# A selective scan's rows of B and C spread by DMA, and five of sixteen products with C moved to GpSimd

## The chip, the core and the metric

The kernel runs on one core of a Trainium2 chip. The metric is the device time of one execution in microseconds (us). A core has five engines that each work through their own instruction list in order and wait for each other by semaphores: TensorE (PE), VectorE (DVE), ScalarE (ACT), GpSimd (POOL) and SyncE (SP), which here only issues DMAs. PE writes to PSUM banks; GpSimd works on SBUF alone.

## The reference, cut to what matters

Six layers run one after another over x of shape (8, 512, 128): a two-of-eight expert layer, attention on sine and cosine features, the expert layer again, a routed attention layer with 16 experts, a selective scan (state space layer), and the routed layer again. The change touches the fifth. For a batch of 512 positions, with 256 inner channels d and 16 states n, it computes

```python
deltaA = jnp.exp(jnp.einsum('bld,dn->bldn', delta, A))
deltaB_u = (delta * u)[..., None] * Bm[:, :, None, :]
def step(h, t):
    dA_t, dBu_t, C_t = t
    h = dA_t * h + dBu_t
    return (h, jnp.einsum('bdn,bn->bd', h, C_t))
```

B, C and a low-rank part of delta come from one product: `inputs @ W_x` gives 64 columns for delta, 16 for B, 16 for C. u is a gated depthwise convolution of the input, and the result is y = sum + u * D, times silu of a second half, times W_out.

## The kernel before, in words

In the scan layer (`scan(4)` in each engine's program) channels lie on partitions, in two halves h of 128, and the 512 positions along the free dimension. The work is cut into units: k = 32 b + 2 s + h for batch b, state s, half h, 256 in all. Each engine's program is a loop over a clock U (`SCAN_CLOCK`, L129), and at each step it issues what is due for units near U, so the order of work is written out by hand. For a unit:

- ScalarE makes the decay exp(dt * A) into a PSUM bank (`decay_of`, L788, one unit ahead; banks `decay`, L334, two of them).
- GpSimd makes dB = du * B into a ring of six SBUF tiles (`dB_of`, L531, three units ahead in its list; `DRING`). It waits for the row of B spread over all partitions, and for the scan six units earlier to have used the slot.
- VectorE scans (`scan_of`, L1544: `tensor_tensor_scan`, h = decay * h + dB, from PSUM and SBUF) into a ring of eight tiles `hs` (`HRING`), and one step later multiplies by C (`times_C`, L1537), which lies spread over partitions in a PSUM bank (`C_bank`), into a ring `hc` of eight.
- PE adds hc into the accumulator of its half (bank 4 or 5) by a product with the identity (`sum_of`, L1180), three units later, or at unit 7 of the batch at the earliest (`sum_at`, L147).

Spreading: a batch's rows of B and C are split by VectorE into three bf16 parts (`three_parts`, L1500 to L1504, front step -5), turned by PE and copied (`bcT3`); for each state PE spreads the row of B into bank 2 by a product with `pick` (`spread_B`, L1157), ScalarE copies it to one of four SBUF tiles `Bs` (`copy_B`, L775, `RING`), and PE spreads the row of C into one of two banks (`spread_C`, L1164).

Beside the units run a batch's preparation (`front`, started a batch or more ahead and spread over the clock: norm at step -13, nmr at -11, u at 0 and 12, dt at 15 and 19, g at 22 and 24; all its products pass through bank 7 one after another, `into_bank7`, L1082) and its end (`back`: yg at 4 and 5, the sum into x at 8; on PE the skip product `skip_u` at 5 and 6 and the output product at 6, `OUT7`). On GpSimd the front holds rstd and two products du (steps -12, 17, 21). The code has a constant `ON_POOL` (L124) for states whose product with C goes to GpSimd; it is empty, so `copy_C` (L781) and GpSimd's `times_C` (L541) run for no state.

In the routed layers, SP spreads rows by DMA: it stores 16 rows to DRAM (`rows_to_dram`, L437) and then reads each into all 128 partitions (`widen`, L441, 256 KB each).

Of the kernel before, what the change touches and what calls it, by code (L numbers as in the profile page):

```python
# [25 lines left out]
NB = 8  # L26
# [97 lines left out]
ON_POOL = ()  # L124
# [17 lines left out]
def copies_C(s):  # L142

    return sum(i % NS in ON_POOL for i in range(s))
# [56 lines left out]
def macaron(nc, x, wl, phase, WqT, bq, WkT, bk, Wv, bv, WoT, bo, gateT, expT, W_in, K_conv, b_conv, W_x,  # L201
            W_dt, b_dt, A_log, D, W_out, b_out, sim, gates, wqkv, wo2, out):
    with ExitStack() as ctx:
# [10 lines left out]
        def plain(name):  # L214
# [109 lines left out]
        rows_sb = [t[0:E2, :] for t in (th, thr)]  # L324
        hs = [sb(f"hs{i}", [P, L]) for i in range(HRING - RING)] + xe
# [8 lines left out]
        decay = [bank[0], bank[6]]  # L334
# [11 lines left out]
        rows_out = plain("rows_out")  # L346
        rows_ps, rows_made = sem("rows_ps"), sem("rows_made")
# [30 lines left out]
            bcT_sb, B_ps, B_sb, C_ps, C_sb, dA_made, dB_made, h_made, hc_dve, hc_pool, hc_used, yg_made = (  # L378
                sem(n) for n in ("nmr_made", "bank7_ps", "rows_read", "dlt_sb", "g_made", "th_made", "thr_made", "u_made", "Du_done", "ez_made",
                                 "ln_made", "dt_made", "gates_made", "bc3_made", "bcT_sb", "B_ps", "B_sb", "C_ps", "C_sb",  # L380
# [37 lines left out]
        def _(sp):  # L418
# [31 lines left out]

            for r in range(2):
                sent = 0
# [13 lines left out]
        def _(pool):  # L466
# [52 lines left out]
            def scan(layer):  # L519
# [11 lines left out]
                def dB_of(k):  # L531
# [4 lines left out]
                    pool.wait_ge(B_sb, seen(s + 1))  # L536
# [4 lines left out]
                def times_C(k):  # L541

                    pool.wait_ge(C_sb, seen(copies_C(k // NH + 1)))
                    pool.wait_ge(h_made, seen(k + 1))
                    if k >= HRING:
                        pool.wait_ge(hc_used, seen(SUM_RANK[k - HRING]))
                    pool.tensor_tensor(hc[k % HRING], hs[k % HRING][:], Cs[copies_C(k // NH) % 2], ALU.mult).then_inc(hc_pool, 1)
# [42 lines left out]
        def _(act):  # L590
# [139 lines left out]
            def scan(layer):  # L730
                def front(b):
# [19 lines left out]
                    act.activation(dlt[0:DR, :], bank[7][0:DR, :], ACT.Copy).then_inc(dlt_sb, 1)  # L751
                    yield
# [22 lines left out]
                def copy_B(s):  # L775
                    act.wait_ge(B_ps, seen(s + 1))
                    if s >= RING:
                        act.wait_ge(dB_made, seen(NH * (s + 1 - RING)))
                    act.activation(Bs[s % RING][:], bank[2][:], ACT.Copy).then_inc(B_sb, 1)

                def copy_C(s):  # L781
                    n = copies_C(s)
                    act.wait_ge(C_ps, seen(s + 1))
                    if n >= 2:
                        act.wait_ge(hc_pool, seen(NH * (n - 1)))
                    act.activation(Cs[n % 2], C_bank[s % 2][:], ACT.Copy).then_inc(C_sb, 1)

# [9 lines left out]
                for U in SCAN_CLOCK:  # L797
                    if 0 <= U + 1 < ALL:
                        decay_of(U + 1)
                    if U % 2 and 0 <= (U + 7) // 2 < NB * NS:  # L800
                        copy_B((U + 7) // 2)
                    due(steps, U)
                    if U % 2 and 0 <= U < ALL and on_pool(U):
                        copy_C(U // 2)
# [8 lines left out]
        def _(pe):  # L813
# [267 lines left out]
            def scan(layer):  # L1081
                def into_bank7(name, b):  # L1082
# [11 lines left out]
                    elif last == "dlt":  # L1094
                        pe.wait_ge(dlt_sb, seen(c + 1))
# [5 lines left out]
                def front(b):  # L1101
# [25 lines left out]
                    pe.matmul(bank[7][0:DR, :], wx_sb[:, 0:DR], xpad[:, 1:L + 1], start=True, stop=True).then_inc(bank7_ps, 1)  # L1127
# [29 lines left out]
                def spread_B(s):  # L1157
                    if s % NS == 0:
                        pe.wait_ge(bcT_sb, seen(s // NS + 1))
                    if s:  # L1160
                        pe.wait_ge(B_sb, seen(s))
                    pe.matmul(bank[2][:], pick[:, s % NS, :], bcT3[s // NS % 2][:], start=True, stop=True).then_inc(B_ps, 1)

                def spread_C(s):  # L1164
                    if s >= 2:
                        last = NH * (s - 1) - 1
                        if on_pool(last):
                            pe.wait_ge(C_sb, seen(copies_C(s - 1)))
                        else:
                            pe.wait_ge(hc_dve, seen(products(last + 1, False)))  # L1170
                    pe.matmul(C_bank[s % 2][:], pick[:, NS + s % NS, :], bcT3[s // NS % 2][:], start=True, stop=True).then_inc(C_ps, 1)  # L1171
# [14 lines left out]
                for U in SCAN_CLOCK:  # L1186
                    if U % 2 == 0 and 0 <= (U + 8) // 2 < NB * NS:
                        spread_B((U + 8) // 2)
# [6 lines left out]
                    if 0 <= U + 1 < ALL and U % 2:  # L1195
                        spread_C((U + 1) // 2)
# [9 lines left out]
        def _(dve):  # L1206
# [283 lines left out]
            def scan(layer):  # L1490
# [46 lines left out]
                def times_C(k):  # L1537
                    dve.wait_ge(h_made, seen(k + 1))
                    dve.wait_ge(C_ps, seen(k // NH + 1))
                    if k >= HRING:  # L1540
                        dve.wait_ge(hc_used, seen(SUM_RANK[k - HRING]))
                    dve.tensor_tensor(hc[k % HRING], hs[k % HRING][:], C_bank[k // NH % 2][:], ALU.mult).then_inc(hc_dve, 1)  # L1542
# [54 lines left out]
```

## Time and profile before

| | us |
|---|---|
| median of 3 runs | 1728.18 (1726.42 to 1730.58) |
| profiled execution | 1722.91 |
| its span | 1721.1 |

| engine | busy us | share of span |
|---|---|---|
| PE | 1474.2 | 86% |
| VectorE | 1208.4 | 70% |
| ScalarE | 585.2 | 34% |
| GpSimd | 435.7 | 25% |

Busy shares are means over stages that have different limits, so the scan stage has to be cut out by time. Its first scan starts at 804.3 us and the last at 1350.6 us. Matmuls are pipelined, so a busy PE need not be at its peak. Times in brackets in a timeline row are the engine's idle time just before and what ended it.

### The profile page before, as it was taken

What the parts mean: (1) busy time and instruction counts of PE and PEld (TensorE: products, weight loads), DVE (VectorE), ACT (ScalarE), POOL (GpSimd) and SP (SyncE); (2) the same over time, 40 slices, a digit from 0 to 9 for tenths busy, and PEclk for the clock granted to TensorE, in tenths of its full rate; (3) what the DMA queues carried; (4) which work ended last, traced back from release to release, by engine and by line L of the source; (5) the groups of instructions that cost most, each with busy time, mean ns of one, the idle gap of its engine ahead of it and who ended that gap; (6) DMA issues with size and microseconds to landing.
All of it is one profiled execution on the core that took longest, in us unless ns stands there. A gap on an engine that the chain in (4) does not pass through costs nothing.

```text
span 1721.1 us, 22005 instructions
## 1 busy us (share of the span) xinstructions
PE 1474.2 (86%) x7582; PEld 1070.7 (62%) x7582; DVE 1208.4 (70%) x2729; ACT 585.2 (34%) x1131; POOL 435.7 (25%) x368
## 2 busy tenths in 40 slices
PE   3997885895999999976888878878887589999998
PEld 3894554795899999842343333333332289999996
DVE  3666663665676666424989898898989767676763
ACT  2203443200222222114646556565565212222221
POOL 1130000001000000004656576565666200000000
PEclk9998997897999999976999989998899889999998
DMA  4000000002232333200000000000000043333330
GB/s 131 1 1 1 1 1 1 1 1 99 99 100 99 101 117 110 70 1 1 0 1 1 1 1 1 0 1 0 1 1 1 6 169 112 121 106 105 105 106 13
DMA packets 49581, 76.76 MB, mean 45 GB/s; under 512 B 6775, under 2 KB 15934, under 8 KB 49342
## 3 DMA queue, kind: packets, MB, share of 16 engines
q1 hardware_dynamic: 49470, 75.35, 13.4%
q8 instruction: 60, 0.98, 0.2%
q14 instruction: 51, 0.42, 0.1%
HBM read 72.71 MB, written 2.62 MB: 44 GB/s over the span
## 4 chain that ended last, share of the span: by engine, by line
PE 63%; DVE 15%; issue 13%; ACT 4%; POOL 3%; DMA 1%; DVEq 0%; POOLq 0%; ACTq 0%
PE bank L1057 20%; PE bank L1060 7%; PE bank L914 5%; PE bank L1183 5%; DVE hs L1550 3%; PE bank L950 2%; PE bank L1017 2%; DVE xe L1550 2%; PE bank L1119 2%; DVE both L1542 2%; PE bank L1002 2%; PE bank L1069 2%; POOL both L539 2%; PE bank L999 1%; PE bank L959 1%
## 5 line engine op out<-in xcount | busy, mean ns | idle before, releaser
L1057 PE MATMUL bank<-wqkv_sb,xe 128*128 128x192 f32 x2048 | 370.4, 334 | 10.5 <-DVE xe L1487 10.3
L1057 PEld LDWEIGHTS bank<-wqkv_sb,xe 128*128 128x128 f32 x2048 | 340.1, 194 | 21.9 <-DVE xe L1487 15.4
L1183 PE MATMUL bank<-both,ident 128*128 128x512 f32 x512 | 265.2, 619 | 3.0 <-DVE both L1542 3.0
L507 POOL TENSOR_TENSOR rstd<-ve,half_neg 128x4 f32<-128x4 f32 x32 | 37.5, 1173 | 769.8 <-DVE ve L1238 769.8
L794 ACT ACTIVATE bank<-dt,A 128x512 f32<-128x512 f32 x256 | 174.5, 687 | 145.2 <-DVE xe L1550 95.0
L539 POOL TENSOR_TENSOR both<-du,prob 128x512 f32<-128x512 f32 x128 | 161.6, 1269 | 102.2 <-DVE xe L1550 56.6
L539 POOL TENSOR_TENSOR both<-du,prT 128x512 f32<-128x512 f32 x128 | 161.5, 1271 | 58.8 <-DVE hs L1550 33.8
L1550 DVE TENSOR_TENSOR_SCAN xe<-bank,both 128x512 f32<-128x512 f32 x128 | 155.3, 1213 | 5.5 <-ACT bank L794 5.2
L1550 DVE TENSOR_TENSOR_SCAN hs<-bank,both 128x512 f32<-128x512 f32 x128 | 155.1, 1212 | 2.1 <-ACT bank L794 2.1
L1183 PEld LDWEIGHTS bank<-both,ident 128*128 128x128 f32 x512 | 97.9, 198 | 86.7 <-issue 54.6
L914 PEld LDWEIGHTS bank<-exp_sb,xe 128*128 128x128 f32 x1024 | 138.3, 197 | 5.0
L914 PE MATMUL bank<-exp_sb,xe 128*128 128x128 f32 x1024 | 138.1, 280 | 0.0
L1060 PEld LDWEIGHTS bank<-wo_sb,xe 128*128 128x128 f32 x1024 | 129.7, 192 | 4.2
L1060 PE MATMUL bank<-wo_sb,xe 128*128 128x128 f32 x1024 | 129.8, 275 | 0.0
L1487 DVE TENSOR_TENSOR xe<-at,bank 128x512 f32<-128x512 f32 x128 | 87.6, 686 | 57.9 <-PE bank L1069 57.5
L1370 DVE TENSOR_TENSOR xe<-both,bank 128x512 f32<-128x512 f32 x128 | 86.7, 684 | 50.3 <-PE bank L906 49.1
L1487 DVE TENSOR_TENSOR xe<-xnT,dt 128x512 f32<-128x512 f32 x128 | 85.4, 688 | 22.4 <-DMA dt<-w_rows 15.7
L1457 DVE TENSOR_REDUCE smax<-bank 128x1 f32<-128x128 f32 (+1 forms) x64 | 31.4, 491 | 98.8 <-PE bank L1002 79.7
L1542 DVE TENSOR_TENSOR both<-hs,bank 128x512 f32<-128x512 f32 x128 | 84.6, 661 | 22.9 <-PE bank L1171 11.2
L710 ACT ACTIVATE prT<-bank 128x128 f32<-128x128 f32 (+1 forms) x64 | 28.0, 437 | 192.9 <-PE bank L1009 192.9
L1487 DVE TENSOR_TENSOR xe<-xnT,du 128x512 f32<-128x512 f32 x128 | 84.5, 687 | 9.3 <-PE bank L1057 8.1
L1542 DVE TENSOR_TENSOR both<-xe,bank 128x512 f32<-128x512 f32 x128 | 84.1, 657 | 0.0
(271 smaller groups left out, 2134.5 us busy)
## 6 DMA issues: line engine op xcount, KB each, us to landing
dt<-w_rows SPq DMA_DIRECT2D x128, 256.0 KB, 4.2
du<-w_rows SPq DMA_DIRECT2D x128, 256.0 KB, 4.9
xs<-in_x_dram SPq DMA_DIRECT2D x8, 256.0 KB, 3.7
out_dram<-xs SPq DMA_DIRECT2D x8, 256.0 KB, 2.5
wqkv_sb<-in_wqkv_dram SPq DMA_DIRECT2D x1, 1536.0 KB
exp_sb<-in_expT_dram SPq DMA_DIRECT2D x1, 512.0 KB, 4.9
wo_sb<-in_wo_dram SPq DMA_DIRECT2D x1, 512.0 KB
win_sb<-in_W_in_dram SPq DMA_DIRECT2D x1, 256.0 KB
```

Of the source, the lines that this page charges most:

```text
L507: pool.tensor_tensor(rstd[:], ve[:], half_neg[:, 0:NT], ALU.pow).then_inc(ln_rstd, 1)
L539: pool.tensor_tensor(dB[k % DRING], du[b % 2][:, h, :], Bs[s % RING][:], ALU.mult).then_inc(dB_made, 1)
L794: act.activation(decay[k % len(decay)][:], dt_[b % 2][:, h, :], ACT.Exp, scale=A[:, h, s:s + 1]).then_inc(dA_made, 1)
L914: m = pe.matmul(bank[7 - b % 2][:, j * P:(j + 1) * P], xe[u % RING][:, j * P:(j + 1) * P], exp_sb[:, e, :], start=(e == 0 and j == 0), sto ...
L950: m = pe.matmul(bank[2 + k % 2][:], feat[:, 2 + c, k * P:(k + 1) * P], feat[:, c, :], start=(c == 0), stop=(c == 1))
L1057: m = pe.matmul(bank[4 + j // 2][:, (j % 2) * 3 * HD:(j % 2 + 1) * 3 * HD], x_e, wqkv_sb[:, e, :], start=(e == 0 and j % 2 == 0), stop=(e ...
L1060: m = pe.matmul(bank[7][:, j * P:(j + 1) * P], x_e, wo2_sb[:, e - E2, :], start=(e == E2 and j == 0), stop=(e == UNIT - 1 and j == NT - 1))
L1183: pe.matmul(bank[4 + k % NH][:], ident[:], hc[k % HRING], start=False, stop=(SUM_RANK[k] == sums_of(k // UNITS, k % NH))).then_inc(hc_used, 1)
L1370: dve.tensor_tensor(xe[u % RING][:], gxT[b], bank[2 + u % 2][:], ALU.mult).then_inc(xe_made, 1)
L1487: dve.tensor_tensor(xe[i % RING][:], xnT[b % 2][:] if e < E2 else at2[:], w, ALU.mult).then_inc(xe_made, 1)
L1542: dve.tensor_tensor(hc[k % HRING], hs[k % HRING][:], C_bank[k // NH % 2][:], ALU.mult).then_inc(hc_dve, 1)
L1550: dve.tensor_tensor_scan(hs[k % HRING][:], decay[k % len(decay)][:], dB[k % DRING], 0.0, ALU.mult, ALU.add).then_inc(h_made, 1)
```

## The change

States 2, 5, 8, 11 and 14 of each batch get their product with C on GpSimd (`ON_POOL`), from SBUF to SBUF; their sums on PE follow six units after the scan instead of three (`sum_at`, unchanged). The product for delta on PE now takes all 96 columns, and ScalarE makes a second copy, of the 32 rows of B and C in fp32, to SBUF (`bc_rows`). SP stores them to DRAM once a batch (`bc_to_dram`) and spreads by DMA each row of B (`widen_B`, four slots `Bs` as before) and the rows of C of the five states (`widen_C`, two slots `Cs`). PE no longer spreads B, and C only for the other eleven states (`spread_C`, banks taken in turn over those states); ScalarE's `copy_B` and `copy_C` go. Bank 2, free now, is a third bank of decay, and ScalarE makes decay two units ahead. VectorE's and PE's counts for C go by the number of states on VectorE. The bf16 split stays, for the eleven states.

```diff
-ON_POOL = ()
+ON_POOL = (2, 5, 8, 11, 14)
...
-        decay = [bank[0], bank[6]]
+        decay = [bank[0], bank[6], bank[2]]
...
+            def bc_to_dram(b):
+                sp.wait_ge(dlt_sb, seen(2 * (b + 1)))
+                sp.dma_start(bc_dram[b], bc_rows).then_inc(bc_out, 16)
+
+            def widen_B(s):
+                b, e = divmod(s, NS)
+                if e == 0:
+                    sp.wait_ge(bc_out, 16 * (b + 1))
+                if s >= RING:
+                    sp.wait_ge(dB_made, seen(NH * (s + 1 - RING)))
+                sp.dma_start(Bs[s % RING][:], bc_dram[b, e:e + 1, :].to_broadcast([P, L])).then_inc(B_in[s % RING], 16)
+
+            def widen_C(s):
+                b, e = divmod(s, NS)
+                n = states_on_pool(s)
+                if n >= 2:
+                    sp.wait_ge(hc_pool, seen(NH * (n - 1)))
+                sp.dma_start(Cs[n % 2], bc_dram[b, NS + e:NS + e + 1, :].to_broadcast([P, L])).then_inc(C_in[n % 2], 16)
+
+            def scan():
+                for U in SCAN_CLOCK:
+                    if (U - 2) % UNITS == 0 and 0 <= (U - 2) // UNITS + 1 < NB:
+                        bc_to_dram((U - 2) // UNITS + 1)
+                    if U % 2 and 0 <= (U + 9) // 2 < NB * NS:
+                        widen_B((U + 9) // 2)
+                    if U % 2 == 0 and 0 <= (U + 6) // 2 < NB * NS and (U + 6) // 2 % NS in ON_POOL:
+                        widen_C((U + 6) // 2)
...
-                    pool.wait_ge(B_sb, seen(s + 1))
+                    pool.wait_ge(B_in[s % RING], 16 * (s // RING + 1))
...
-                    pool.wait_ge(C_sb, seen(copies_C(k // NH + 1)))
+                    n = states_on_pool(k // NH)
+                    pool.wait_ge(C_in[n % 2], 16 * (n // 2 + 1))
...
                     act.activation(dlt[0:DR, :], bank[7][0:DR, :], ACT.Copy).then_inc(dlt_sb, 1)
+                    if b:
+                        act.wait_ge(bc_out, 16 * b)
+                    act.activation(bc_rows, bank[7][DR:W3, :], ACT.Copy).then_inc(dlt_sb, 1)
...
-                    if 0 <= U + 1 < ALL:
-                        decay_of(U + 1)
-                    if U % 2 and 0 <= (U + 7) // 2 < NB * NS:
-                        copy_B((U + 7) // 2)
+                    if 0 <= U + 2 < ALL:
+                        decay_of(U + 2)
                     due(steps, U)
-                    if U % 2 and 0 <= U < ALL and on_pool(U):
-                        copy_C(U // 2)
...
                     elif last == "dlt":
-                        pe.wait_ge(dlt_sb, seen(c + 1))
+                        pe.wait_ge(dlt_sb, seen(2 * (c + 1)))
...
-                    pe.matmul(bank[7][0:DR, :], wx_sb[:, 0:DR], xpad[:, 1:L + 1], start=True, stop=True).then_inc(bank7_ps, 1)
+                    pe.matmul(bank[7][0:W3, :], wx_sb[:], xpad[:, 1:L + 1], start=True, stop=True).then_inc(bank7_ps, 1)
...
-                def spread_B(s):
+                def spread_C(s):
+                    d = states_on_dve(s)
                     if s % NS == 0:
                         pe.wait_ge(bcT_sb, seen(s // NS + 1))
...
-                    pe.matmul(C_bank[s % 2][:], pick[:, NS + s % NS, :], bcT3[s // NS % 2][:], start=True, stop=True).then_inc(C_ps, 1)
+                    if d >= 2:
+                        pe.wait_ge(hc_dve, seen(NH * (d - 1)))
+                    pe.matmul(C_bank[d % 2][:], pick[:, NS + s % NS, :], bcT3[s // NS % 2][:], start=True, stop=True).then_inc(C_ps, 1)
...
-                    if U % 2 == 0 and 0 <= (U + 8) // 2 < NB * NS:
-                        spread_B((U + 8) // 2)
...
-                    if 0 <= U + 1 < ALL and U % 2:
+                    if 0 <= U + 1 < ALL and U % 2 and not on_pool(U + 1):
                         spread_C((U + 1) // 2)
```

## Rows read from the trace of the kernel before

**Rows 1.** Busy us (instructions) by stretch: PE, PEld, DVE, ACT, POOL, clock, DMA, GB/s.

```profile
804.00:1351.00 547.00, 456.19 (x1204) 189.55 (x1202) 500.89 (x683) 310.58 (x508) 337.96 (x270) 0.92 0.00 1
1085.00:1154.00 69.00, 57.97 (x163) 24.66 (x162) 64.35 (x92) 40.66 (x68) 43.69 (x36) 0.95 0.00 1
```

**Rows 2.** VectorE's waits in the scan stage: total us, times, longest.

```profile
DVE both L1542 <- PE bank L1171: 11.2, 4, 3.0
DVE u L1510 <- ACT th L744: 8.6, 8, 1.9
DVE both L1542 <- DVE hs L1550: 5.9, 7, 0.9
DVE both L1542 <- issue: 5.8, 3, 2.2
DVE xe L1550 <- ACT bank L794: 5.2, 7, 0.7
...
DVE hs L1550 <- ACT bank L794: 2.1, 4, 0.6
```

**Rows 3.** Timeline of VectorE, mid-stage: start us, length us, what.

```profile
1098.77 1.21 DVE L1550 TENSOR_TENSOR_SCAN xe<-bank,both 128x512 f32<-128x512 f32 x1
1099.91 0.66 DVE L1542 TENSOR_TENSOR both<-xe,bank 128x512 f32<-128x512 f32 x1
1100.49 1.21 DVE L1550 TENSOR_TENSOR_SCAN hs<-bank,both 128x512 f32<-128x512 f32 x1
```

**Rows 4.** Groups by form, 873 to 1293 us: busy us, mean ns, idle before.

```profile
L539 POOL TENSOR_TENSOR both<-du,prob 128x512 f32<-128x512 f32 x96 | 121.3, 1269 | 79.7 <-DVE xe L1550 46.0 <-DVE hs L1550 33.7
...
L779 ACT ACTIVATE prob<-bank 128x512 f32<-128x512 f32 x48 | 28.1, 585 | 46.1 <-PE bank L1162 46.0
```

**Rows 5.** GpSimd's waits in the scan stage, and three dBs in a row (timeline).

```profile
POOL rstd L507 <- DVE ve L1238: 26.1, 6, 4.4
POOL du L528 <- DVE dt L1518: 18.0, 8, 2.4
...
1053.08 3.73 POOL L539 TENSOR_TENSOR both<-du,prT 128x512 f32<-128x512 f32 x3
```

**Rows 6.** A crowded stretch behind a batch's end, and TensorE's timeline in it.

```profile
1096.50:1113.50 17.00, 17.00 (x53) 8.04 (x52) 13.44 (x17) 5.84 (x11) 9.75 (x8) 0.95 0.00 1
...
1109.92 0.38 PE L1162 MATMUL bank<-bcT,pick 96*128 96x512 bf16 x1
1110.13 1.02 PE L1183 MATMUL bank<-both,ident 128*128 128x512 f32 x2
1110.99 1.88 PE L1119 MATMUL bank<-xpad,wcv 128*128 128x512 f32 x4
```

**Rows 7.** Three small VectorE operations in the stage: ns min/median/max, first and last.

```profile
L1265 DVE CAST bc<-bc_r x7: 226/226/1172, 801.7 to 1219.0; 128x128 bf16<-128x128 f32 x7
L1266 DVE TENSOR_TENSOR bc_r<-bc_r,bc x7: 292/293/1251, 802.9 to 1219.3; 128x128 f32<-128x128 f32 x7
L1497 DVE SCALAR_TENSOR_TENSOR nmr<-mv,rstd x8: 163/263/1215, 755.8 to 1205.3; 128x4 f32<-128x4 f32 x8
```

**Rows 8.** Timeline at the stage's first split of B and C.

```profile
801.34 2.63 POOL L539 TENSOR_TENSOR both<-du,prT 128x512 f32<-128x512 f32 x2
801.66 1.17 DVE L1265 CAST bc<-bc_r 128x128 bf16<-128x128 f32 x1
802.86 1.25 DVE L1266 TENSOR_TENSOR bc_r<-bc_r,bc 128x128 f32<-128x128 f32 x1
```

**Rows 9.** Timeline of GpSimd just behind a later batch's split.

```profile
1148.53 1.27 POOL L539 TENSOR_TENSOR both<-du,prob 128x512 f32<-128x512 f32 x1 [2.54 <-DVE xe L1550]
```

**Rows 10.** The routed layers' row transfers (L449), issue to landing.

```profile
DMA to landing us min/median/max: 3.0/4.3/7.3
```

**Rows 11.** Stretches with one grstd of GpSimd each, with and without DMA.

```profile
12.20:15.20 3.00, 0.00 (x0) 0.00 (x0) 0.02 (x1) 0.00 (x0) 2.91 (x1) 1.00 0.81 211
...
279.00:282.10 3.10, 0.00 (x0) 0.00 (x0) 0.04 (x1) 0.00 (x0) 2.90 (x1) 0.50 0.00 0
```

**Rows 12.** GpSimd's first dBs of the stage.

```profile
796.27 4.94 POOL L539 TENSOR_TENSOR both<-du,prob 128x512 f32<-128x512 f32 x4 [4.01 <-ACT prob L779]
```

More of the change, by code:

```diff
@@ L139, in products, with states_on_dve, states_on_pool @@
     return sum(on_pool(i) == pool for i in range(k))
-def copies_C(s):
+def states_on_dve(s):
+    return s - states_on_pool(s)
+def states_on_pool(s):
     return sum(i % NS in ON_POOL for i in range(s))
@@ L324, in macaron @@
         rows_sb = [t[0:E2, :] for t in (th, thr)]
+        bc_dram = nc.dram_tensor("bc_dram", [NB, 2 * NS, L], F32).ap()
+        bc_rows = xnT[0][0:2 * NS, :]
         hs = [sb(f"hs{i}", [P, L]) for i in range(HRING - RING)] + xe
@@ L346, in macaron @@
         rows_out = plain("rows_out")
+        bc_out = plain("bc_out")
+        B_in = [plain(f"B_in{i}") for i in range(RING)]
+        C_in = [plain(f"C_in{i}") for i in range(2)]
         rows_ps, rows_made = sem("rows_ps"), sem("rows_made")
@@ L377, in macaron @@
         nmr_made, bank7_ps, rows_read, dlt_sb, g_made, th_made, thr_made, u_made, Du_done, ez_made, ln_made, dt_made, gates_made, bc3_made, \
-            bcT_sb, B_ps, B_sb, C_ps, C_sb, dA_made, dB_made, h_made, hc_dve, hc_pool, hc_used, yg_made = (
+            bcT_sb, C_ps, dA_made, dB_made, h_made, hc_dve, hc_pool, hc_used, yg_made = (
                 sem(n) for n in ("nmr_made", "bank7_ps", "rows_read", "dlt_sb", "g_made", "th_made", "thr_made", "u_made", "Du_done", "ez_made",
-                                 "ln_made", "dt_made", "gates_made", "bc3_made", "bcT_sb", "B_ps", "B_sb", "C_ps", "C_sb",
+                                 "ln_made", "dt_made", "gates_made", "bc3_made", "bcT_sb", "C_ps",
                                  "dA_made", "dB_made", "h_made", "hc_dve", "hc_pool", "hc_used", "yg_made"))
@@ L449, in widen @@
                 sp.dma_start(wide[n % SLOTS], w_rows[r * NB + c, e:e + 1, :].to_broadcast([P, L])).then_inc(wide_in[n % SLOTS], 16)
+            def bc_to_dram(b):
[22 more added lines that the diff above has]
+                        widen_C((U + 6) // 2)
             for r in range(2):
+                if r:
+                    scan()
                 sent = 0
@@ L546, in times_C @@
                         pool.wait_ge(hc_used, seen(SUM_RANK[k - HRING]))
-                    pool.tensor_tensor(hc[k % HRING], hs[k % HRING][:], Cs[copies_C(k // NH) % 2], ALU.mult).then_inc(hc_pool, 1)
+                    pool.tensor_tensor(hc[k % HRING], hs[k % HRING][:], Cs[n % 2], ALU.mult).then_inc(hc_pool, 1)
                 steps = on_clock(front, (-12, 17, 21))
@@ L773, in front @@
                         yield
[L775 to L786, printed above, removed]
                 def decay_of(k):
@@ L1155, in back @@
                     yield
-                def spread_B(s):
+                def spread_C(s):
+                    d = states_on_dve(s)
                     if s % NS == 0:
                         pe.wait_ge(bcT_sb, seen(s // NS + 1))
[L1160 to L1170, printed above, removed]
-                    pe.matmul(C_bank[s % 2][:], pick[:, NS + s % NS, :], bcT3[s // NS % 2][:], start=True, stop=True).then_inc(C_ps, 1)
+                    if d >= 2:
+                        pe.wait_ge(hc_dve, seen(NH * (d - 1)))
+                    pe.matmul(C_bank[d % 2][:], pick[:, NS + s % NS, :], bcT3[s // NS % 2][:], start=True, stop=True).then_inc(C_ps, 1)
                 def skip_u(b, h):
@@ L1538, in times_C @@
                     dve.wait_ge(h_made, seen(k + 1))
-                    dve.wait_ge(C_ps, seen(k // NH + 1))
+                    d = states_on_dve(k // NH)
+                    dve.wait_ge(C_ps, seen(d + 1))
                     if k >= HRING:
                         dve.wait_ge(hc_used, seen(SUM_RANK[k - HRING]))
-                    dve.tensor_tensor(hc[k % HRING], hs[k % HRING][:], C_bank[k // NH % 2][:], ALU.mult).then_inc(hc_dve, 1)
+                    dve.tensor_tensor(hc[k % HRING], hs[k % HRING][:], C_bank[d % 2][:], ALU.mult).then_inc(hc_dve, 1)
                 def scan_of(k):
```

## The prediction

> **What bounds the kernel now.** I first read the busy table by stretch [rows 1]. The scan stage runs from 804 to 1351 us, 547 us of the 1721.1 us span, for eight batches of 32 units (16 states times two channel halves): 70 us a batch. Outside it the diff changes nothing but the first 50 us of the stage. In it VectorE is busy 500.9 us (92%), TensorE 456, GpSimd 338, ScalarE 311. So VectorE sets the pace: per unit a scan and a product with C. The timeline [rows 3] gives their pitch, start to start: scan to product 1.14 us, product to the next scan 0.58 us, 1.72 us a unit, 55 us a batch. The other 15 us are side work (norm, u, dt, g, the batch's end) and waits.
>
> Second, VectorE's waits in the stage [rows 2]: 11.2, 5.9 and 5.8 us before products, 8.6 before u, 7.3 (5.2 and 2.1) before scans, for ScalarE's decay. Those before products and u lie just behind a batch's end, when TensorE has u's skip product, the output product and five held-back sums to do at once: in 1096.5 to 1113.5 it is busy 17.00 of 17 us [rows 6]. Third, GpSimd's waits [rows 5]: 26.1 us for the norm's variance, 18.0 for dt, and otherwise for VectorE's scans, since the dB ring of six is full. GpSimd has room: 43.7 us of work in a batch of 69 [rows 1].
>
> **The change, part by part.** I sum against the profiled execution, 1722.9 us, 1.8 above its span and 5.3 under the median of the three runs, 1728.2.
>
> *Products off VectorE.* Ten products of a batch (states 2, 5, 8, 11, 14), 80 in all, at 0.58 us of pitch [rows 3]: **-46.4 us**, all on VectorE's path, if scans run at 1.14 us behind one another. That pair is not in the trace; the pitch scan to product is its nearest row, as both leave the scan's drain behind.
>
> *On GpSimd* they cost 80 of the 1.27 us operation [rows 4], 1.24 us in a row (3 in 3.73 us, [rows 5]). A batch then holds 45 such operations, 56 us, and about 1 us of rstd: 57 us, under VectorE's batch below. In six units GpSimd has eight operations, 9.9 us; VectorE six scans and four products, 9.2 us, and on average 1.7 us of side work (70 - 55 - 5.8 us idle, a batch). So it falls back in stretches and catches up behind side work, with a ring of six to draw on. Cost on the path 0 while that holds. Its products wait for scans that the dB before them already waited for, and the sums move three units later for them; scan k+8 needs product k, which stands in front of dB(k+8) in GpSimd's order anyway.
>
> *What GpSimd does to VectorE's small operations.* The rows show a cost that the idle GpSimd now avoids. Two of VectorE's operations with both ends or both inputs in SBUF, the cast bc and the subtraction bc_r, take 0.23 and 0.29 us, but once 1.17 and 1.25; nmr takes 0.26 and once 1.22 [rows 7]. The long ones lie at 801.66 and 802.86, while GpSimd works back to back [rows 8]; in a steady batch GpSimd is waiting for a scan 2.54 us long there [rows 9] and nothing is lost. After the change GpSimd is backlogged there: at step 27 (the split of B and C into three bf16 parts) it still owes product 23 and dB 31 to 33, four operations, 5 us, against 1.8 us of split. As in the start, I take two long operations and nmr: 0.95 + 0.96 + 0.96 = 2.9 us, in the six batches with a split and nmr: **+17 us**. Bounds: 0 (GpSimd waits there as today) and five operations of the split, seven of the norm and nmr, 13 at 0.96 us, 75 us. Scans, products, u, dt, g have one operand in PSUM, and scan and product keep 1.21 and 0.66 us beside a busy GpSimd [rows 3]: no loss there. The Trainium skill, page "SBUF — State Buffer", section "Who interferes with whom", says that VectorE and GpSimd share one port pair, locked for a whole instruction, against VectorE operations with two SBUF inputs or in a 2-port mode, and that a VectorE operation with one SBUF input doesn't contend. The trace agrees; by the rule without these rows I would only know that some operations wait for up to one of GpSimd's.
>
> *Decay in three banks, B's copies gone.* ScalarE loses 16 copies of 0.585 us a batch [rows 4] and gains one, for the rows of B and C, and may be one unit further ahead. It was not the bound; of VectorE's 7.3 us for decay [rows 2] I take **-5** (0 to -7.3). The extra copy sits between the dlt product and bcT, which have over 20 units until batch b+1 needs them: 0, at most 8 x 0.6 = +5.
>
> *TensorE* loses 21 spreads of a batch at 0.21 us and keeps sums at 0.86 us [rows 6]. In the crowded stretch that is four spreads of B and one of C, 1.1 us, and the sum of unit 4 moves out of the burst: 0.86. So the stretch shrinks from 17 to 15.0 us and VectorE's own work in it by three products, 1.7 us: the wait of about 3.5 us stays, 0.3 us shorter: 7 x 0.3 = **-2** (-6 to +4, if the late sum doesn't help).
>
> *Rows by DMA.* SP issues 21 transfers of 256 KB a batch, some 85 GB/s. The same form of transfer (one row to 128 partitions) lands in 3.0 to 7.3 us, median 4.3 [rows 10]. A B slot is free once dB(2s-7) is done and is wanted by dB(2s), six operations on, 7.4 us at the least, 10 with products between. So 0; if each came at 7.3 us plus an issue, under 1 us a state would show. The added waits: GpSimd's on B stands ahead of the dBs, all of which scans need; ScalarE's on the store of the batch before, a batch old when it comes; TensorE's on both copies of dlt holds the sums of units -1 on by up to 0.6 us, as in the bound above. Each C has eleven dBs of time. On SP's queue the store of the rows waits for ScalarE's copy at unit 1 to 2, and behind it stand B of states 6 on, which dB(12) needs: about four units of slack. That DMA slows GpSimd is not in the rows: grstd takes 2.91 us with the DMA engines 81% busy and 2.90 with none [rows 11].
>
> *The start.* GpSimd's first dB now waits 4.01 us for ScalarE's copy of B [rows 12]. With B there early its ring fills before the first split: **-2** (the two long operations go), scan 0 hangs on the split. *The end:* the last pool product may hold the last sum, **+1** (0 to 3).
>
> Sum: -46.4 + 17 - 5 - 2 - 2 + 1 = -37.4; 1722.9 - 37.4 = 1685.5, and 5.3 on top for the median: **1691 us**, 2.1% faster. VectorE's batch would be about 65.5 us.
>
> **Rivals.**
> A. *No collision.* GpSimd still waits for scans at the split and at nmr. For it: today's 2.54 us of waiting [rows 9]. Against: ten more operations a batch, four owed at that step. Time 1691 - 17 = 1674.
> B. *GpSimd becomes the second bound.* Its waits for variance and dt, 26.1/6 + 18.0/8 = 6.6 us a batch [rows 5], don't shrink, so that it needs 57 + 6.6 + 1.5 (blocked by VectorE's operations) = 65 us and alternates with VectorE: scans wait for dB now and then, 67.5 us a batch instead of 65.5. Then 1691 + 8 x 2 = 1707. For it: GpSimd is slower than VectorE over six units. Against: both waits arise because it is ahead, and go as it falls back.
> C. *Slower: the shared operations.* If all 13 small operations of a batch wait for GpSimd: 1691 - 17 + 75 = 1749. The point from which this makes the kernel slower is ten long ones a batch (54 us gained without them, by 6 x 0.96). Against: GpSimd itself waits for the norm's result, so it runs dry during the norm.
> D. *The rows come late,* SP's order holding them behind the store: dB waits as today's scan waits don't. If one batch's three states lose 3 us each in seven batches: +63, 1754. Against: slack of four units.
> E. *It doesn't do what it says:* the products go, but TensorE's in-order queue, waiting for GpSimd's late sums, gives C late, so that VectorE idles where the products were: within 0.2%. Sums stand six units behind and GpSimd is at most about four late.
>
> **How the numbers follow.** Chances: forecast (1682 to 1700) 0.47, A 0.18, B 0.20, C 0.05, D 0.05, E 0.05. A difference under 0.2% (3.5 us) can't be told from none here. Faster: forecast, A, B: 0.85; same 0.05; slower 0.10. The range leaves out C to E and a little more: 1669 (A with the lower bounds of decay and TensorE) to 1715 (B with the upper bounds of the small terms).
>
> **What would show it.** Right: a stage of about 512 us instead of 547; 176 products left on VectorE and 80 on GpSimd at 1.27 us; scans 1.14 us apart where a product is gone; bc and bc_r operations of about 1.2 us in most batches (A: 0.3 us); GpSimd over 85% busy with its waits for variance and dt shrunk (B: not shrunk, and scans released by dB); no wait of GpSimd on a DMA but at the start; VectorE's waits for decay near none, and TensorE again full for 15 us behind each batch's end. Wrong if scans behind scans take over 1.2 us, if GpSimd's operation grows beside the DMA, or if GpSimd waits for B.

## The result, and the profile after

The changed kernel takes 1680.39 us (median of 4 runs, 1677.74 to 1686.56) against 1727.3 (1726.29 to 1730.58) for the kernel before on the same chip: ratio 0.9733, 95% interval 0.9715 to 0.9751. It is 46.9 us faster, where 37 were forecast. The profiled execution took 1677.74 us, with a span of 1675.6.

The scan stage by stretches (columns as in [rows 1]): the whole stage, the 15 us behind one batch's end (from the start of yg), and that batch whole.

```profile
803.00:1303.00 500.00, 416.52 (x1038) 175.24 (x1036) 466.15 (x601) 247.31 (x389) 430.85 (x350) 0.91 0.29 86
1071.80:1086.80 15.00, 14.78 (x51) 7.09 (x50) 13.33 (x16) 5.85 (x9) 12.93 (x11) 1.00 0.40 112
1071.80:1136.60 64.80, 54.14 (x142) 23.33 (x141) 61.02 (x83) 32.59 (x52) 55.45 (x46) 0.92 0.33 85
```

From first to last scan start the stage takes 499.6 us instead of 546.3: -46.7, the whole gain. VectorE works 466 us instead of 501 (-34.7) and idles 33.9 instead of 46.1 (-12.2). GpSimd is busy 86% of the stage.

VectorE's and GpSimd's waits in the stage, total us, times, longest; they answer [rows 2] and [rows 5].

```profile
DVE u L1526 <- ACT th L784: 20.1, 7, 5.4
DVE both L1559 <- issue: 6.1, 6, 1.0
DVE both L1559 <- PE bank L1189: 1.9, 1, 1.9
DVE both L1559 <- DVE hs L1567: 1.7, 3, 0.7
DVE xs L1550 <- PE bank L1178: 1.3, 1, 1.3
...
POOL rstd L546 <- DVE ve L1254: 11.4, 6, 1.9
POOL du L567 <- DVE dt L1534: 9.3, 6, 1.6
```

The kernel before has one more wait in its stage that [rows 2] leaves out:

```profile
DVE xs L1534 <- PE bank L1152: 5.2, 4, 1.6
```

VectorE's waits before products fell from 22.9 to 9.7 us (all of their releasers together), before the sum xs from 5.2 to 1.3, before scans from 7.3 to none; those before u rose from 8.6 to 20.1. No wait of GpSimd on a DMA stands in the list.

Three scans in a row on VectorE's timeline (start us, length us), and the split's operations by tile (ns min/median/max, first and last start), to be held against [rows 3] and [rows 7].

```profile
1031.88 3.44 DVE L1567 TENSOR_TENSOR_SCAN hs<-bank,both 128x512 f32<-128x512 f32 x3
...
L1279 DVE CAST bc<-bc_f x7: 226/594/3215, 801.5 to 1182.0; 128x128 bf16<-128x128 f32 x7
L1280 DVE TENSOR_TENSOR bc_r<-bc_f,bc x7: 293/1251/1257, 801.8 to 1182.6; 128x128 f32<-128x128 f32 x7
L1281 DVE CAST bc<-bc_r x7: 226/1173/1180, 802.1 to 1183.9; 128x128 bf16<-128x128 f32 x7
L1282 DVE TENSOR_TENSOR bc_r<-bc_r,bc x7: 292/293/1256, 802.4 to 1185.1; 128x128 f32<-128x128 f32 x7
...
L1513 DVE SCALAR_TENSOR_TENSOR nmr<-mv,rstd x6: 262/268/272, 846.1 to 1171.2; 128x4 f32<-128x4 f32 x6
```

### The profile page after: what moved, and what is told of

Same layout as the page of the kernel before. It is cut to its first block, busy times and chain, and to the rows that moved or that the text cites. A ratio compares the mean times of both kernels' runs of the same rounds, so it can differ in the third digit from the quotient of the medians.

```text
span 1675.6 us, 21605 instructions
## 1 busy us (share of the span) xinstructions
PE 1433.5 (86%) x7414; PEld 1056.8 (63%) x7414; DVE 1171.5 (70%) x2649; ACT 521.5 (31%) x1011; POOL 528.3 (32%) x448
## 3 DMA queue, kind: packets, MB, share of 16 engines
q1 hardware_dynamic: 74046, 119.93, 22.9%
## 4 chain that ended last, share of the span: by engine, by line
PE 68%; DVE 17%; issue 8%; POOL 4%; ACT 2%; DMA 1%; DVEq 0%; POOLq 0%; ACTq 0%
PE bank L1083 21%; PE bank L1086 7%; PE bank L1201 7%; PE bank L940 5%; PE bank L1145 3%; DVE xe L1567 2%; PE bank L976 2%; DVE both L1559 2%; PE bank L1043 2%; DVE hs L1567 2%; PE bank L1028 2%; POOL both L578 2%; PE bank L1095 2%; PE bank L1025 2%; PE bank L985 1%
## 5 line engine op out<-in xcount | busy, mean ns | idle before, releaser
L1083 PEld LDWEIGHTS bank<-wqkv_sb,xe 128*128 128x128 f32 x2048 | 339.1, 194 | 21.4 <-DVE xe L1503 14.9
L1201 PE MATMUL bank<-both,ident 128*128 128x512 f32 x512 | 267.6, 651 | 17.8 <-DVE both L1559 16.8
L1201 PEld LDWEIGHTS bank<-both,ident 128*128 128x128 f32 x512 | 104.8, 211 | 151.9 <-issue 108.1
L578 POOL TENSOR_TENSOR both<-du,prob 128x512 f32<-128x512 f32 x128 | 161.0, 1269 | 34.8 <-DVE xe L1567 20.1
L1386 DVE TENSOR_TENSOR xe<-both,bank 128x512 f32<-128x512 f32 x128 | 86.7, 684 | 50.5 <-PE bank L932 49.3
L1503 DVE TENSOR_TENSOR xe<-xnT,dt 128x512 f32<-128x512 f32 x128 | 85.3, 688 | 23.0 <-DMA dt<-w_rows 15.9
L1559 DVE TENSOR_TENSOR both<-hs,bank 128x512 f32<-128x512 f32 x96 | 63.4, 661 | 9.7 <-issue 6.1
L1145 PE MATMUL bank<-xpad,wcv 128*128 128x512 f32 x128 | 68.6, 667 | 0.0
```

The lines of the kernel that those rows point to most:

```text
L578: pool.tensor_tensor(dB[k % DRING], du[b % 2][:, h, :], Bs[s % RING][:], ALU.mult).then_inc(dB_made, 1)
L1083: m = pe.matmul(bank[4 + j // 2][:, (j % 2) * 3 * HD:(j % 2 + 1) * 3 * HD], x_e, wqkv_sb[:, e, :], start=(e == 0 and j % 2 == 0), stop=(e ...
L1145: m = pe.matmul(bank[7][:], wcv[:, tap, h * P:(h + 1) * P], xpad[:, tap:tap + L], start=False, stop=(tap == 3))
L1201: pe.matmul(bank[4 + k % NH][:], ident[:], hc[k % HRING], start=False, stop=(SUM_RANK[k] == sums_of(k // UNITS, k % NH))).then_inc(hc_used, 1)
L1386: dve.tensor_tensor(xe[u % RING][:], gxT[b], bank[2 + u % 2][:], ALU.mult).then_inc(xe_made, 1)
L1503: dve.tensor_tensor(xe[i % RING][:], xnT[b % 2][:] if e < E2 else at2[:], w, ALU.mult).then_inc(xe_made, 1)
```

## Experiments

Each was timed beside the kernel before, and its ratio is against that. Times are medians; the stage is first to last scan start. The runs come from several chips, on which the kernel before took 1725.1 to 1727.94 us, so a difference between two experiments can be off by 1 to 3 us.

**One part alone.** The changed kernel without GpSimd's products (rows by DMA and third bank stay):

```diff
-ON_POOL = (2, 5, 8, 11, 14)
+ON_POOL = ()
```

> The changed kernel with no state on GpSimd: all 256 products on VectorE again, B's rows still by DMA, three banks of decay. Theory: the products are worth 80 x 0.60 = 48 us, of which the longer operations of VectorE's bf16 split give 15 back; without both: 1680 + 48 - 15 = 1713, the split's four long operations at 0.29 us or (the first cast) 0.67 us again, and VectorE's idle time in the stage about 12 us under that of before, since that part of the gain belongs to DMA and decay. Rival: the drop in VectorE's idle time came with the products (fewer spreads of C, sums moved out of the burst), so that DMA and decay alone give little: 1722 to 1727.

Measured 1714.75 us (1710.84 to 1714.98), ratio 0.993 (0.9912 to 0.9949). That is near the theory's 1713. The split's second and third operations are back at 0.29 and 0.23 us, and no scan waits for decay. Then the kernel before with the same constant set to the five states, and nothing else:

> The kernel before with only the states set: states 2, 5, 8, 11, 14 on GpSimd, B and these C spread by TensorE and copied by ScalarE (21 copies a batch), two banks of decay, no DMA. Theory: products -48, split +15, so 1727 - 33 = 1694; ScalarE has 40.7 + 5 x 0.58 us a batch of 65 and stays hidden, with 7 to 10 us of VectorE waits for decay. Rival: ScalarE's copies in order before the decays and TensorE's spreads delay the scans and dB, which is what the DMA was for: 1705 or more, with VectorE waits on decay over 20 us.

Measured 1708.01 us (1704.02 to 1710.39), ratio 0.9889 (0.9867 to 0.9911): 14 above the one theory, as the rival had it (its "over 20 us" of waits on decay came out as 19.6). Its waits in the stage:

```profile
DVE u L1510 <- ACT th L744: 24.7, 11, 3.1
DVE hs L1550 <- ACT bank L794: 11.6, 14, 2.4
DVE xe L1550 <- ACT bank L794: 8.0, 14, 0.8
...
POOL both L547 <- ACT qk_sb L786: 26.0, 14, 5.0
POOL both L547 <- ACT at L786: 23.3, 15, 5.0
```

GpSimd waits 49.3 us for ScalarE's copies of C, and scans wait 19.6 us for decay. Against 1727.3 us the parts alone bring 12.6 and 19.3 us, 32 together; both bring 46.9. The remaining 15 belong to the pair: with rows by DMA, ScalarE has no copies of C and B in front of the decay that the faster VectorE asks for. The next experiment bears this out: with the same five states and the same two banks, but rows by DMA, scans wait 7.1 us for decay instead of 19.6.

**Two decay banks in the changed kernel.**

```diff
-        decay = [bank[0], bank[6], bank[2]]
+        decay = [bank[0], bank[6]]
...
-                    if 0 <= U + 2 < ALL:
-                        decay_of(U + 2)
+                    if 0 <= U + 1 < ALL:
+                        decay_of(U + 1)
```

> The changed kernel with the third bank of decay taken back: two banks, ScalarE one unit ahead as before. Theory (the forecast's term for decay, seen in full in the trace of after): VectorE waited 7.3 us before scans for the decay in the kernel before and 0 now; this comes back, perhaps a little more because scans now follow each other at 1.12 us: 1680 + 7 = 1687, with some 7 to 12 us of waits of VectorE on the decay in the trace. Rival: with B's copies gone from ScalarE (128 copies at 0.58 us) the decay is in time with two banks as well, the third bank is worth nothing: 1680, waits of VectorE on the decay under 1 us.

Measured 1700.42 us (1697.3 to 1702.07), ratio 0.985 (0.9832 to 0.9869): the third bank is worth 20 us, not 7. VectorE's waits of this kernel:

```profile
DVE u L1526 <- ACT th L784: 20.1, 7, 5.4
DVE both L1559 <- PE bank L1189: 7.9, 4, 2.1
DVE xs L1550 <- PE bank L1178: 6.1, 4, 1.9
DVE xe L1567 <- ACT bank L824: 5.1, 7, 0.8
...
DVE hs L1567 <- ACT bank L824: 2.0, 4, 0.5
```

Decay itself accounts for 7.1. A second part lies behind the batches' ends. The granted clock in the 15 us behind six ends is 1.00, 1.00, 0.77, 1.00, 0.89 and 0.77, where the changed kernel has 1.00 in all six. At the three ends at 1.00 VectorE waits before xs and products as in the changed kernel (1.02 us); at the other three it waits 4.0, 2.5 and 4.1 us there, 7.5 us more together. That raised the question of TensorE's clock, which had no term in the prediction.

**The split read from PSUM.** VectorE's three-part split takes its input from bank 7 and leaves the rest there, instead of in SBUF; so no operation of it has both ends or both inputs in SBUF.

```diff
-                    dve.tensor_copy(bc_f[:], bank[7][:, 0:NT * 32].rearrange("p (j e) -> p j e", e=32)).then_inc(rows_read, 1)
-                    dve.wait_ge(rows_read, seen(b + 1))
...
-                    three_parts(bc_f[:], bc_r[:], bc3, 32, bc3_made)
+                    rows7, rest7 = (bank[7][:, i * NT * 32:(i + 1) * NT * 32].rearrange("p (j e) -> p j e", e=32) for i in range(2))
+                    three_parts(rows7, rest7, bc3, 32, bc3_made)
```

> The changed kernel with VectorE's bf16 split of B and C reading its fp32 rows and keeping its rests in the PSUM bank they arrive in (bank 7), so that each of its operations has at most one operand in SBUF to read; the same five steps, the copy before them gone, bank 7 held 1.5 us longer. Theory: the split's operations grow from 0.23 and 0.29 us to about 1.2 because they meet GpSimd's operations at a shared way into SBUF, and only when both their inputs, or their input and output, are in SBUF; here they stay under 0.4 us beside a GpSimd as busy as now: -15 us of length and -2 of the copy and cast, 1680 - 15 = 1665. Rival: they wait for something else that came with the change (the DMAs writing SBUF, the semaphores), and stay long: 1680.

Measured 1681.31 us (1678.64 to 1682.88), ratio 0.974 (0.9722 to 0.9759): no gain. But the operations did become short, beside an equally busy GpSimd. The split by tile; one batch by stretches, with the 15 us behind its end first; and the timeline behind that end.

```profile
L1280 DVE TENSOR_TENSOR bank<-bank,bc x7: 299/299/300, 807.3 to 1187.1; 128x128 f32<-128x128 f32 x7
L1281 DVE CAST bc<-bank x7: 291/291/292, 807.6 to 1187.4; 128x128 bf16<-128x128 f32 x7
...
1073.70:1088.70 15.00, 13.78 (x37) 7.29 (x38) 10.90 (x14) 3.98 (x7) 10.23 (x10) 0.77 0.34 96
1073.70:1138.50 64.80, 54.39 (x140) 24.29 (x140) 57.80 (x81) 32.69 (x53) 55.20 (x46) 0.92 0.29 87
...
1074.52 1.10 PE L1196 MATMUL bank<-u,Dmat 128*128 128x512 f32 x2 [2.51 <-DVE both L1546]
1078.75 3.78 PE L1178 MATMUL bank<-wout_sb,both 128*128 128x128 f32 x16
1082.57 0.69 DVE L1549 TENSOR_TENSOR xs<-xs,bank 128x512 f32<-128x512 f32 x1 [1.94 <-PE bank L1178]
1086.54 0.69 DVE L1558 TENSOR_TENSOR both<-hs,bank 128x512 f32<-128x512 f32 x1 [2.16 <-PE bank L1189]
```

VectorE works 57.8 us of a batch instead of 61.0, and the batch stays at 64.8. The theory's 1665 us failed, though its cause of the long operations held. The 3.2 us are lost behind the end: TensorE idles 2.51 us before the skip product, waiting for yg, then gets a clock of 0.77 over the 15 us (two stretches of 2 us in it at 0.50, half speed, 1.2 GHz), and VectorE waits for it before xs and before products, 14.5 and 14.8 us in all; from yg to u it idles 6.5 us at each end instead of 3.5. All six ends look like this. In the changed kernel TensorE waits for yg 0.2 us or less at such an end (0.9 and 1.0 at the first two). There TensorE has fallen to half speed already, *before* the end, behind an idle stretch of 3.19 us in which it waits for u:

```profile
1129.87 2.02 PE L1153 MATMUL bank<-xpad,wx_sb 128*96 128x512 f32 x2 [3.19 <-DVE u L1526]
...
1120.00:1128.00 8.00, 5.14 (x13) 1.80 (x11) 7.93 (x10) 3.17 (x5) 6.32 (x6) 1.00 0.36 101
1128.00:1130.00 2.00, 0.13 (x1) 0.13 (x2) 2.00 (x4) 0.69 (x1) 2.00 (x3) 0.77 0.45 119
1130.00:1132.00 2.00, 2.00 (x3) 0.92 (x4) 2.00 (x3) 0.07 (x1) 2.00 (x3) 0.50 0.00 0
...
1136.60:1151.60 15.00, 14.82 (x51) 7.11 (x50) 13.29 (x16) 5.85 (x9) 12.95 (x11) 1.00 0.36 119
```

The same idle stretch of 3.19 us and the half speed behind it lie ahead of all six ends. TensorE works at half speed where VectorE's own work covers it, has little idle time left before the end, and is at 1.00 (2.4 GHz) when the crowded work comes. If so, filling that idle time in the kernel above should bring the 16 us that were missing.

**A filling product.** Three products nobody reads, into the free bank 7, before the skip product at unit 5 of batches 1 to 6:

```diff
+                        if U % UNITS == 5 and h == 0 and UNITS <= U < ALL - UNITS:
+                            pe.wait_ge(bcT_sb, seen(U // UNITS + 2))
+                            for _ in range(3):
+                                pe.matmul(bank[7][:], ident[:], xpad[:, 1:L + 1], start=True, stop=True)
```

> f4_split_from_psum with three products on TensorE (identity by the batch's padded input, 0.86 us each at full clock, into bank 7, which is free there and overwritten by the output product) put ahead of the skip product at unit 5 of batches 1 to 6; they add 15.5 us of useless TensorE work. In f4 VectorE's split was 3.2 us a batch shorter and its waits behind the batch's end 3.2 us longer: TensorE stood idle 2.5 us before the skip product, its granted clock fell to 0.50 for the next 7 us, and the output product took 3.78 us instead of 2.05. Theory: the idle stretch and the clock behind it ate f4's gain. With the idle time filled the crowded stretch runs at clock 1.0, VectorE's waits there fall by about 3 us a batch, and the time is 1681 - 6 x 3 = 1663. Rival: the batch is paced by something that neither kernel changed (its length is 64.8 us in both), such as TensorE's total work: the added products make it slower, 1681 to 1696.

Measured 1665.46 us (1663.12 to 1667.03), ratio 0.9639 (0.9617 to 0.9662): 15.9 us off (17 by the ratios), by adding work to TensorE alone, as the theory had it. The clock is 1.00 behind all six ends; behind one of them:

```profile
1062.20:1077.20 15.00, 14.60 (x47) 6.66 (x46) 13.29 (x16) 4.36 (x7) 12.94 (x11) 1.00 0.31 95
```

The same filling in the kernel with two decay banks, and in the changed kernel itself:

> f1_two_banks (the changed kernel with two banks of decay, 1700 us) with the three filling products of h1_fill ahead of the skip product. f1 lost 20 us where 7 to 12 were expected; VectorE's waits for the decay came back as 7 us, and in four of seven batches the clock was at 0.50 to 0.60 behind the batch's end, which it isn't in the profile of the changed kernel. Theory: the other 13 us are the clock; with TensorE kept busy ahead of the burst the time is 1700 - 11 = 1689, with the clock at 1.0 behind the batches' ends. Rival: two banks cost 20 us in another way (ScalarE late for bank 7's work); the fill changes nothing or adds TensorE work: 1700 to 1705.

Measured 1694.0 us (1690.44 to 1695.63), ratio 0.9816 (0.9793 to 0.9839). The clock is 1.00 behind all six ends, and 6 of the 13 us beyond decay's own waits are back, near the 7.5 us that the three slow ends had lost. The other 7 stay open.

> The changed kernel with the three filling products. Theory: in its profile TensorE waits 0.3 us or less for yg before the burst and the clock is at 1.0 there (the fall lies ahead, and the slow stretch fills the idle time), so that there is nothing to gain: the fill's 2.6 us a batch are paid where TensorE was late: 1680 to 1690. Rival: the fill helps as in h1_fill, since it moves the clock's fall away from the whole end of the batch: 1668.

Measured 1688.04 us (1686.65 to 1692.87), ratio 0.9783 (0.976 to 0.9806): 8 us *slower* than without. Where TensorE has hardly any idle time, the products only stand in the way; VectorE's waits before products rose from 9.7 to 17.2 us, 13.2 of them for spread C.

**The wait for u.** It is the largest left: 2.45 us in each of six batches, 5.42 once. The six lie in the crowded stretch too, 16.8 us behind yg. ScalarE waits for TensorE's second convolution product, which is issued two steps before its use. The first run is a probe of the time alone: it leaves out two of that product's four taps, so that its output is not the reference's.

> The changed kernel with two of the four taps of the convolution's second half left out (a probe: 1.7 us of TensorE work less in the crowded stretch behind each batch's end, the output is not the reference's for those channels). Theory: VectorE's waits for u (20.1 us over the stage, 2.45 a batch) are TensorE being full for 16 us behind each batch's end; they fall by 1.7 us in each of seven batches, so that the time is 1680 - 12 = 1668, unless the clock takes it back. Rival: VectorE waits for u because ScalarE's tanh stands behind decays in its list; the waits stay at 20 us, 1680.

Measured 1671.96 us (1671.0 to 1675.27), ratio 0.9677 (0.9657 to 0.9697). The u waits fell from 20.1 to 9.2 us; of these 10.9, 8.4 came out as time. Next, the same product moved ahead of the crowded stretch, with all its work (FRONT7 and PE step of conv1 from 8 to 3, its second half to 4; ScalarE's step 11 to 6; VectorE's u 12 to 7; the output product 6 to 8, xs 8 to 10):

> The changed kernel with other places on the clock: the convolution's second half at units 3 and 4 instead of 8 and 10, its tanh at 6 and u at 7, the output product at 8 instead of 6 and the sum into x at 10. It moves 3.7 us of TensorE work from behind the batch's end to ahead of it, where TensorE waited for yg. Theory (TensorE's burst is what VectorE waits for there, 3.5 us a batch): the waits for u and for C go, -3 us a batch: 1680 - 7 x 3 = 1659. Rival: the batch's end moves behind the convolution and the sums pile up instead, or VectorE's waits come back as waits for dB, since GpSimd is busy 55.4 of 64.8 us: 1675 to 1690.

Measured 1673.33 us (1671.51 to 1677.37), ratio 0.9685 (0.9663 to 0.9707): between the theories. u waits only at the start (4.2 us, 15.9 less in all). But VectorE's waits before products rose from 9.7 to 16.4 us and those before g from 0.7 to 2.2, so that about 8 us are left of it. VectorE still works 61.1 us of a 64.8 us batch, since the split is as long as in the changed kernel (some 24 us in six batches, now mostly in its first cast). So the last kernel does both, this order and the split from PSUM:

> h3_conv_early and f4_split_from_psum together: the convolution early and the split out of SBUF. Theory: with TensorE's burst gone VectorE is the bound over the whole batch, and now the 3.2 us a batch of the split show as well: 3 us a batch from each, 1680 - 21 - 19 = 1640, with GpSimd's waits for scans under 3 us a batch. Rival: GpSimd, with 45 operations at 1.24 us, 57 us a batch and its waits for the variance and dt (3.5 us), binds at 61 us: 1650 or more, with scans released by dB.

Measured 1642.49 us (1640.47 to 1644.46), ratio 0.9503 (0.9483 to 0.9524), 38 us under the changed kernel, near the theory's 1640 and the fastest of all. One batch:

```profile
1056.30:1114.30 58.00, 50.68 (x142) 22.46 (x141) 57.55 (x81) 32.87 (x53) 55.17 (x46) 0.97 0.37 98
```

VectorE works 57.55 of 58.00 us and GpSimd 55.17. VectorE's waits before products are down to 4.1 us in the stage. Neither step alone brings this (7 us for the order, nothing for the split), and together they bring more than their sum. Alone, the gain came back as other waits of VectorE: all of it behind the ends with the split from PSUM, about half before products and g with the order.

**A sixth state on GpSimd,** in that kernel:

```diff
-ON_POOL = (2, 5, 8, 11, 14)
+ON_POOL = (1, 4, 6, 9, 12, 14)
```

> h4_both with six states on GpSimd (1, 4, 6, 9, 12, 14) instead of five. Theory: h4's batch is 58.0 us, VectorE busy 57.55 of it and GpSimd 55.2; two more products take 1.2 us off VectorE and put 2.5 on GpSimd, 57.7 us plus 1 of rstd's wait and some idle: GpSimd becomes the bound and the batch about 59.5 us, 1642 + 12 = 1654. Rival: the 1.2 us of VectorE show, since GpSimd's waits for the variance shrink in turn: 1642 - 8 = 1634.

Measured 1663.73 us (1660.53 to 1666.41), ratio 0.9637 (0.9615 to 0.9658): 21 us slower than with five, slower than either theory says. GpSimd is busy 57.6 of 63 us, and no scan waits for dB, so the reason given for a loss is not it either. VectorE's waits lie before products (11.8 us), xs (10.3), u (10.0, of which 5.9 at the start) and the split (5.6), mostly for TensorE's results, and the clock over a batch is 0.89 instead of 0.97. What starts it was not settled; here the pattern of the states was changed together with their number.

## Why the prediction was right, and where its sum was off

*Direction, size, bound.* VectorE's work was the bound, and taking 80 products off it gave the gain. The measured 1680.39 us lies in the outer range (1669 to 1715), 11 us under the middle and 1.6 under the forecast's own band (1682 to 1700). By the number alone rival A (1674) is nearer, though its mechanism, no collision, did not occur. The range was also a little narrower than its stated parts: A with the lower bounds gives 1668, B with the upper bounds of decay, TensorE and the end 1720. The sum said -37.4, and the stage gave -46.7. The terms:

| term | forecast | measured | from |
|---|---|---|---|
| products | -46.4 | -48.4 | three scans in 3.44 us: 1.12 apart, a product 0.60 |
| collision | +17 | +14.9 | split 10.3 to 25.2 us in six batches, nmr none |
| decay | -5 | -7.3 | no wait left |
| TensorE: products and xs | -2 | -17.1 | waits before products 22.9 to 9.7, before xs 5.2 to 1.3 |
| TensorE: u | in the above | +7.9 | u's waits, without the start |
| start | -2 | +2.1 | u's wait 3.6 longer, scan 0 1.5 earlier |
| end | +1 | +1.7 | last scan to xs, 6.17 to 7.87 us |

They add up to -46.2; the span fell by 45.5, and 0.7 us of waits before g are new. TensorE's two rows together are -9.2 against the -2 that was forecast. The misses of the products, collision and decay (6 us together) and of TensorE (7) went the same way, the start's 4 us the other way: that the sum is only 9 us off owes that much to luck.

*Products: right*, 2 us short. After a scan the next scan starts 0.02 us sooner than a product does.

*Collision: right in mechanism and size, wrong in which operations.* The subtraction of 0.29 us takes 1.25 and the cast of 0.23 takes 1.17 in five of six batches, as [rows 7] had it once; in the sixth the first cast takes 3.21 us instead. The forecast had two long ones in the split and nmr. Measured, the split loses 2.5 us a batch, against 1.91 forecast for it, and nmr nothing: it keeps 0.27 us in all six batches. The long nmr of [rows 7], 1.22 us, started at 791.07 us, ahead of the stage; the six in the stage took 0.26 in the kernel before as well. The timeline shows a long subtraction held until the operation that GpSimd had started before it ends:

```profile
1052.92 1.26 POOL L578 TENSOR_TENSOR both<-du,prT 128x512 f32<-128x512 f32 x1
1053.07 1.26 DVE L1280 TENSOR_TENSOR bc_r<-bc_f,bc 128x128 f32<-128x128 f32 x1
```

The kernel with its split from PSUM shows the cause: same sizes, same GpSimd, operands moved, 0.30 and 0.29 us. The Trainium skill ("SBUF — State Buffer", section "Who interferes with whom") gives the rule for this, an exclusive lock of the port pair that VectorE and GpSimd share; here it held, and the measured 1.25 us fits one of GpSimd's 1.27 us operations. That the remedy alone brings no time is the part no term of mine had.

*Decay: right in kind, undersized.* The 7.3 us of waits went, where 5 were taken. Removing the bank from the changed kernel costs 20 us, since its loss also disturbs TensorE's work behind the batch ends (6 us shown by the filling, 7 open).

*TensorE: the step that failed.* The term was forecast at -2, with -6 as its bound, and measured at -9.2. I shortened the crowded stretch by 2 us of work and left "the wait of about 3.5 us" in place. Both the stretch and the wait were read at one batch's end [rows 6]. Six ends of before, read by their granted clock, would have shown that this one is no typical case; here are two others, 15 us from yg:

```profile
880.80:895.80 15.00, 13.42 (x38) 6.97 (x38) 11.04 (x15) 4.96 (x9) 7.26 (x6) 0.77 0.01 2
1163.20:1178.20 15.00, 14.20 (x37) 7.58 (x37) 10.46 (x14) 4.37 (x8) 7.24 (x6) 0.67 0.00 0
```

The six clocks before are 0.77, 0.77, 0.89, 0.89, 0.67 and 0.77; after, 1.00 in all. VectorE's idle time from yg to u goes with them: 5.8, 5.7, 4.0, 3.6, 6.4 and 5.8 us before, 5.2 on average, and 3.5 at each of the six ends after. So the wait that stays was rightly put at about 3.5 us; the wait that the kernel before had was put too low, since the batch that was read (the fourth, 3.6 us) is the least of the six. The difference over six ends, 10.4 us, is the miss; waits elsewhere take 1 us of it back.

The timeline says where the clock's place moved. In the kernel before TensorE idles 3.1 us just ahead of its skip product, waiting for yg, and half speed (0.50) lies behind yg at all six ends; after, it lies ahead of yg at all six. That a clock at half speed there costs VectorE this time is shown by the filling product (0.77 to 1.00, 15.9 us), in the kernel with its split from PSUM. That it is the whole of the change's extra gain is argued, not shown: no filling was run in the kernel before.

The rise before u has another cause. VectorE's operations there that had to wait, before (three lines) and after (two lines):

```profile
1105.79 0.69 DVE L1542 TENSOR_TENSOR both<-hs,bank 128x512 f32<-128x512 f32 x1 [1.78 <-issue]
1110.17 0.69 DVE L1542 TENSOR_TENSOR both<-hs,bank 128x512 f32<-128x512 f32 x1 [0.85 <-DVE hs L1550]
1113.54 0.69 DVE L1510 SCALAR_TENSOR_TENSOR u<-th,bank 128x512 f32<-128x512 f32 x1 [0.97 <-ACT th L744]
...
1081.50 0.69 DVE L1559 TENSOR_TENSOR both<-hs,bank 128x512 f32<-128x512 f32 x1 [1.02 <-issue]
1088.60 0.69 DVE L1526 SCALAR_TENSOR_TENSOR u<-th,bank 128x512 f32<-128x512 f32 x1 [2.45 <-ACT th L784]
```

From the first of them to u pass 7.75 us before, 1.82 of them idle (0.85 and 0.97), and 7.10 after, 2.45 of them idle, at all six ends. So VectorE's own work shrank by 1.3 us, and the time until TensorE's product has passed through ScalarE only by 0.65. The 7.10 and 2.45 us stand unchanged in the kernel with the split from PSUM (clock 0.77 behind the ends) and in the one with the filling (1.00). The lower clock ahead of the end is therefore not what makes u wait; this is the wait for TensorE's own work that the forecast left in place.

*Start: wrong.* The first split did become short, 0.23 and 0.29 us, and scan 0 came earlier. But u(0) followed at 809.48 instead of 807.37: TensorE ran its eight convolution products in 6.74 us at a clock of 0.59, and u hangs on those, not on dB.

*Rows by DMA: right.* 256 KB land in 3.3 us (median) at 86 GB/s, nothing waits for them, and GpSimd's operation keeps its 1.27 us beside them.

*Rivals.* A (no collision) falls by the split's rows. B (GpSimd as second bound) falls: no scan waits for dB, and GpSimd's waits for variance and dt shrank from 44.1 to 20.7 us as it fell back. C falls: of the 13 operations only four of the split's grow; the norm's keep their 0.15 to 0.17 us. D and E don't occur: GpSimd waits for no DMA, and the products' time came off.

## What to carry to other kernels

When the bound engine gets faster, look at the engine that serves it in bursts: read its granted clock and the bound engine's idle time behind every burst's start, before pricing them from one. Work moved to GpSimd blocked VectorE's small SBUF operations here, for one of its operations or for several in a row; keep their source and rest in PSUM, and judge it only together with the next wait in line. Where TensorE idles just before its densest stretch, a product that nobody reads can pay for itself, and where it doesn't idle the same product costs.

## What the runs showed of the hardware

At the batch ends read here TensorE at half speed came behind an idle stretch of some us, and slowed the work that followed: 3.19 us of idle time, then 0.50 for about 6 us (about 3 at the first two ends); 2.51 us, then 0.50 from 1077 to 1082 us. Three added products, 2.77 us together, kept it at 1.00.

A small VectorE operation can wait for more than one of GpSimd's. In the kernel before with GpSimd's products alone, the split's first cast (0.23 us at its shortest) takes 3.79 us in the median of six batches: it stands until three operations of GpSimd, issued one after another, are done. The timeline of the first of them (start us, length us):

```profile
863.06 3.86 DVE L1263 CAST bc<-bc_f 128x128 bf16<-128x128 f32 x1
863.10 1.29 POOL L539 TENSOR_TENSOR both<-du,prT 128x512 f32<-128x512 f32 x1
864.32 2.52 POOL L539 TENSOR_TENSOR both<-du,prob 128x512 f32<-128x512 f32 x2
```

A price of one GpSimd operation for each collision, as in my sum, is therefore no upper bound.
